# Sandwich block on eight cores: two router loads queued behind two weight slabs, and the second layer norm written into the projection's buffer

## The reference

```python
x = x + _layernorm(_L0_attn_ref(_layernorm(x), Wq, Wk, Wv, Wo))
x = x + _layernorm(_L0_ffn_ref(_layernorm(x), base_W, router_W, lora_A, lora_B))

# attention: Q = x @ Wq.T (32 heads of 128), K = x @ Wk.T, V = x @ Wv.T (one head),
# rotary embedding, windows of 512 tokens that overlap by half:
scores = jnp.einsum('bhqd,bkd->bhqk', Qw, Kw) * scale
attn = jax.nn.sigmoid(scores)
attn = attn / jnp.sum(attn, axis=-1, keepdims=True)
wout = jnp.einsum('bhqk,bkd->bhqd', attn, Vw)      # overlapping windows are blended linearly
return out @ Wo.T

# feed-forward: 8 experts, top 2, adapters of rank 16
base = jnp.einsum('bsd,od->bso', x, base_W)
logits = jnp.einsum('bsd,ed->bse', x, router_W)    # softmax, top 2, renormalised: w_dense
mid = jnp.einsum('bsd,edr->bser', x, lora_A) * w_dense[..., None]
inc = jnp.einsum('bser,erd->bsd', mid, lora_B)
return base + inc * SCALING
```

## Time and profile before

| | |
|---|---|
| median of 3 runs | 2698.13 us (2696.24 to 2703.28) |
| profiled execution, its time | 2701.05 us |
| profiled execution, span of the slowest core (core 4) | 2699.2 us |
| spans of the other cores | 2678.3 to 2691.7 us |
| TensorE matmul, busy | 1951.5 us (72%) |
| ScalarE, busy | 657.0 us (24%) |
| VectorE, busy | 603.9 us (22%) |
| DMA queue of GpSimd | 113.35 MB, 36.3% of the 16 DMA engines' time |

### The profile page before, as it was taken

One profiled execution on the slowest core, in us unless ns is written; L12 is line 12 of the kernel. 1 busy time (PEld: TensorE's weight loads), 2 busy tenths in 40 slices (PEclk: granted clock), 3 DMA queues, 4 the chain that ended last, 5 costly groups with the idle time before them and its releaser, 6 DMA issues.

```text
span 2699.2 us, 49584 instructions; the slowest of 8 cores (2678.3 to 2699.2 us)
## 1 busy us (share of the span) xinstructions
PE 1951.5 (72%) x20000; PEld 1667.1 (62%) x20000; DVE 603.9 (22%) x1752; ACT 657.0 (24%) x1143; POOL 101.9 (4%) x82
## 2 busy tenths in 40 slices
PE   1357999999977777772999999722125999999400
PEld 0237999999755555552888888621124888888400
DVE  2431222222134434431000000133432000000244
ACT  3650111111254554550011111133232111111111
POOL 1000000000000000000000000000000000000000
PEclk9999999999988988885999999855556999999755
DMA  9821445654200000006576776412152676676233
GB/s 201 197 94 33 64 63 75 83 64 64 32 2 2 2 2 2 2 2 53 60 89 68 79 79 70 71 33 63 48 83 43 71 87 70 72 85 71 85 148 140
DMA packets 228587, 178.96 MB, mean 66 GB/s; under 512 B 18960, under 2 KB 222736, under 8 KB 222736
## 3 DMA queue, kind: packets, MB, share of 16 engines
q0 software_dynamic: 217568, 113.35, 36.3%
q1 hardware_dynamic: 10800, 62.45, 6.4%
HBM read 263.97 MB, written 25.17 MB: 107 GB/s over the span
## 4 chain that ended last, share of the span: by engine, by line
PE 64%; DVE 12%; ACT 9%; issue 8%; DMA 7%; DVEq 1%; ACTq 0%; SPq 0%; POOL 0%; POOLq 0%
PE ps_all L768 17%; PE ps_all L653 17%; PE ps_all L443 16%; PE ps_all L541 5%; DVE bn L263 5%; DMA xstage<-x_ext 3%; ACT sig L508 2%; PE ps_all L494 2%; DMA out<-outstage 2%; DMA slab<-woT 2%; DVE bl L575 1%; DVE outstage L794 1%; PE ps_all L295 1%; ACT xt_stage L282 1%; PE ps_all L677 1%
## 5 line engine op out<-in xcount | busy, mean ns | idle before, releaser
L653 PE MATMUL ps_all<-slab,attn_T 128*128 128x256 bf16 x4096 | 449.5, 273 | 46.6 <-DMA slab<-woT 46.6
L443 PE MATMUL ps_all<-slab,ln1T_own 128*128 128x256 bf16 x4096 | 469.6, 273 | 0.6 <-ACT krT L374 0.6
L768 PE MATMUL ps_all<-slab,ln2T 128*128 128x256 bf16 x4096 | 464.0, 274 | 0.2 <-issue 0.2
L653 PEld LDWEIGHTS ps_all<-slab,attn_T 128*128 128x128 bf16 x4096 | 401.9, 98 | 94.1 <-issue 46.7
L768 PEld LDWEIGHTS ps_all<-slab,ln2T 128*128 128x128 bf16 x4096 | 402.1, 98 | 48.1 <-issue 0.3
L443 PEld LDWEIGHTS ps_all<-slab,ln1T_own 128*128 128x128 bf16 x4096 | 396.3, 98 | 45.0 <-issue 0.8
L508 ACT ACTIVATE sig<-ps_all,kbias_s 128x512 bf16<-128x512 f32 x384 | 225.5, 722 | 228.1 <-PE ps_all L494 228.0
L541 PE MATMUL ps_all<-v_sb,sig 128*128 128x128 bf16 x2048 | 204.3, 229 | 75.3 <-DVE bl L584 70.0
L541 PEld LDWEIGHTS ps_all<-v_sb,sig 128*128 128x128 bf16 x2048 | 192.3, 108 | 85.4 <-issue 85.1
L551 PE MATMUL ps_all<-onesc,sig 128*128 128x1 bf16 x2048 | 199.3, 175 | 0.0
L494 PE MATMUL ps_all<-qrT,krT 128*128 128x256 bf16 x768 | 153.3, 317 | 39.7 <-ACT sig L508 35.5
(11 more groups left out here) (86 smaller groups left out, 1494.1 us busy)
## 6 DMA issues: line engine op xcount, KB each, us to landing
slab<-wqT POOLq DMA_DIRECT2D x16, 2048.0 KB, 17.5
slab<-woT POOLq DMA_DIRECT2D x16, 2048.0 KB, 21.9
slab<-baseT POOLq DMA_DIRECT2D x16, 2048.0 KB, 18.8
xstage<-x_ext SPq DMA_DIRECT2D x12, 2048.0 KB, 14.7
out<-outstage SPq DMA_DIRECT2D x8, 2048.0 KB, 6.7
xre<-x_ext POOLq DMA_DIRECT2D x8, 1024.0 KB, 9.9
x_scratch<-x1b SPq DMA_DIRECT2D x8, 1024.0 KB, 4.3
x1re<-x_scratch SPq DMA_DIRECT2D x8, 1024.0 KB, 4.9
```

What stands on the lines that cost most here:

```text
L443: return e.matmul(reg, ln1T_own[:, d, t * 128:(t + 1) * 128], slabs[par][:, d, :], start=(d == 0), stop=(d == 31))
L653: return e.matmul(reg, attn_T[:, d, t * 128:(t + 1) * 128], slabs[par][:, d, :], start=(d == 0), stop=(d == 31))
L768: return e.matmul(reg, ln2T[:, d, t * 128:(t + 1) * 128], slabs[par][:, d, :], start=(d == 0), stop=False)
```

## The change

Two edits. The loads of a_all and routerT leave the place between C and D and are issued on GpSimd after the loads of woT slabs 0 and 1 and before that of slab 2; a_all still waits for C_DONE, routerT follows it in order. FW2_N, the value that the router's matmuls wait for, is the same 32 as before. And E's second layer norm writes into proj[:, t, :], tile t's own part of the projection, instead of xt2stage, which is gone; the wait for earlier transposes to be evicted goes with it.

```diff
-    xt2stage= sb("xt2stage", (128, D), BF16, FREG + 8192)
@@
     s_fw2 = P.sem("s_fw2")
-    P.op("gpsimd", lambda e: e.dma_start(
-            out=a_all_s[:, :, :],
-            in_=a_all.rearrange("(t p) c -> p t c", p=128)),
-         waits=[(s_ate, C_DONE)], inc=s_fw2, inc_by=16)
-    P.op("gpsimd", lambda e: e.dma_start(
-            out=routerT_s[:, :, :],
-            in_=routerT.rearrange("(t p) c -> p t c", p=128)),
-         waits=[(s_ate, C_DONE)], inc=s_fw2, inc_by=16)
-    FW2_N = s_fw2.n
+    FW2_N = 32
 
     p_ring = Ring([ps[0], ps[1], ps[2], ps[3]], init_conds=[(s_ate, C_DONE)])
     pev_counts = {}
     for s in range(NSLAB):
         par, c_slab = emit_slab_load(woT, s)
+        if s == 1:
+            P.op("gpsimd", lambda e: e.dma_start(
+                    out=a_all_s[:, :, :],
+                    in_=a_all.rearrange("(t p) c -> p t c", p=128)),
+                 waits=[(s_ate, C_DONE)], inc=s_fw2, inc_by=16)
+            P.op("gpsimd", lambda e: e.dma_start(
+                    out=routerT_s[:, :, :],
+                    in_=routerT.rearrange("(t p) c -> p t c", p=128)),
+                 inc=s_fw2, inc_by=16)
@@
-        c_ap2 = emit_ln_stats_apply(x1b[tp][:, :], xt2stage[:, :],
-                                    waits=[(s_chain, c_add)],
-                                    extra_apply_waits=[(s_tpe, s_tpe.n)])
+        c_ap2 = emit_ln_stats_apply(x1b[tp][:, :], proj[:, t, :],
+                                    waits=[(s_chain, c_add)])
@@
-        emit_transpose_tile(xt2stage[:, :], dvf, src_waits=[(s_apply, c_ap2)])
+        emit_transpose_tile(proj[:, t, :], dvf, src_waits=[(s_apply, c_ap2)])
```

## The result

| | before | changed |
|---|---|---|
| median of 8 runs | 2697.69 us | 2656.71 us (2654.24 to 2660.46) |
| profiled execution, its time | 2701.05 us | 2656.56 us |
| its span, slowest core | 2699.2 us | 2655.0 us |

The ratio of the times is 0.9848, with a 95% interval of 0.9837 to 0.9859: 41 us less. The forecast was 46.1 us less, so it was right in kind and 5 us too large. The ratio, and every time and ratio of the experiments, leaves out executions in which a die was disturbed; one such is among the eight behind 2697.69, which without it would be 2697.26.

The account below looks back on a forecast made before the run. It took the join of C and D as the bound: slab 0's load queued behind a_all, which waits for C. Terms 45.65 + 0.5 + 0 = 46.1 us brought the median from 2698.13 to 2652.0; range 2646 to 2661.

Parts of the forecast that it names:

- (1): Ahead of stage D on core 4: slabs 0 and 1 load under C at no cost, removing 45.65 us.
- one sign of being wrong in kind: Stage C, the attention: growth by more than a microsecond or two would show the prediction wrong in kind.
- (2): Slab 2's load in D: queue empty 6 us before its issue, 5 us of slack, cost nothing.
- The rival's price of 13.8 us: Stage D: slab 2 lands late behind routerT, TensorE waits 13.8 us, time 2666; chance 0.09.
- the 28 that the prediction named: Loads in stage D: landing times should stay under 28 us after issue.
- (3): D's entry: TensorE's clock still starts low, no gain taken; bounds 2.7 us gained, about 1 us lost.
- The sum: Whole kernel on core 4: 45.65 + 0.5 + 0 = 46.1 us gained, median 2652.0.
- core 4 stays the slowest: End of the kernel: core 4 still ends last, narrowly, with core 6 at 2651.0, 2 us below it.
- the forecast had 0.5: Stage E's second layer norm: 8 applies each lose 0.06 us of wait handling, 0.5 us gained.
- the gain is that of another core: Stall ahead of D: if a core with core 6's 41.2 us is slowest, gain 40.8, time 2657; chance 0.10.

Follow-up runs that it names:

- e5: The changed kernel with each of the two early woT slab loads done seven times under the attention; 2653.9 us, ratio 0.985.
- e8: The changed kernel with a_all and routerT held until slab 0 is multiplied, issued directly ahead of slab 2; 2661.3 us, ratio 0.988.
- e10: The changed kernel with tile t+1's layer norms issued inside tile t's router work, but xt2stage and its wait kept; 2559.2 us, ratio 0.9504.
- e2: The changed kernel with a_all and routerT back ahead of slab 0, so only the layer norm's buffer edit remains; 2691.2 us, ratio 0.9988.
- e6: The changed kernel with a_all alone back ahead of slab 0, routerT after slab 1; 2686.2 us, ratio 0.997.
- e7: The changed kernel with routerT alone back ahead of slab 0, a_all after slab 1; 2685.7 us, ratio 0.9969.
- e4: The changed kernel with slabs 0 and 1 also waiting for the attention's end, still ahead of the router loads; 2678.4 us, ratio 0.9941.

## Why the prediction was right, and where 5 us went

*The stall goes whole* ((1) of the prediction): right. The new gap is 1.1 us; 1241.75 - 1240.80, the end of C's last matmul, had allowed 0.95. Transfers under C cost nothing that can be told, shown at seven times the traffic. The prediction had named one sign of being wrong in kind, an attention longer by more than a microsecond or two. Core 4 showed it, with 4.9 us; the mean of the eight cores, 509.0 against 509.2, and e5 say that it was that core's scatter.

*Slab 2* ((2)): right. No wait of line 653 for a slab is left, and D's loads on core 4 landed in time:

```profile
DMA to landing us min/median/max: 16.7/17.3/18.1
```

The working was cautious: routerT landed 12.1 us after its issue, not 22.5, so the queue was empty 17 us ahead of slab 2 and not 6. The rival's price of 13.8 us was too high; e8 put it at 8.0, a wait of 5.5 and 2.5 of slow clock, which the price had left out. The slack is not large, though: in e10 one core's loads took up to 28.5 us to land in D, past the 28 that the prediction named, and it waited 1.5 us for a slab. No other core of the runs with the new order (but for e8) waited for one.

*The clock* ((3)): right. Windows of the changed kernel at D's entry, beside the earlier trace rows; the clock stands after POOL's busy time.

```profile
1244.00:1246.00 2.00, 0.43 (x3) 0.29 (x3) 1.30 (x6) 0.13 (x1) 0.00 (x0) 0.99 0.00 0
1246.00:1248.00 2.00, 0.92 (x6) 0.49 (x5) 0.19 (x1) 1.06 (x2) 0.14 (x1) 0.50 0.00 0
1248.00:1250.00 2.00, 2.00 (x12) 1.37 (x10) 0.00 (x0) 0.00 (x0) 2.00 (x2) 0.50 0.00 0
1250.00:1252.00 2.00, 2.00 (x11) 1.40 (x10) 0.00 (x0) 0.00 (x0) 1.21 (x1) 0.50 0.03 3
1252.00:1254.00 2.00, 2.00 (x17) 1.61 (x16) 0.00 (x0) 0.11 (x1) 0.00 (x0) 0.81 1.29 106
1254.00:1256.00 2.00, 2.00 (x21) 1.79 (x19) 0.00 (x0) 0.27 (x1) 0.00 (x0) 1.00 1.80 179
```

D starts at 0.50 (1.2 GHz) again and reaches 1.00 (2.4 GHz) after some 6 us. TensorE had been busy for 0.43 of the 2 us ahead of the fall. The ramp comes with the attention's thin end even without the stall; 449.8 us of matmuls in D against 449.5 say the same. The Trainium skill's rule (TensorE: Matmul & The Clock Gate, "HAM oscillation — how this bites in real kernels"), that avoiding the idle gap avoids the ramp, isn't borne out at D's entry: the gap went from 46.6 to 1.1 us and the ramp stayed. The other half of it, that a gap brings the ramp, e8 shows, where dense matmuls lay ahead of waits of 4.0 and 6.9 us.

*The sum*: here the size was off. It took core 4's 46.6 us, the longest stall of the eight in one execution, as the stall of whichever core ends last, and held that "core 4 stays the slowest". It did in the profiled pair, whose times differ by 44.5 us. That close agreement is partly luck: core 4's D began only 39.7 us earlier, and stage E (3.0 us, of which the forecast had 0.5) and what follows F's slab matmuls (1.7 us) happened to be shorter in the second profile. But in 13 timed executions of the kernel before, the slowest core was 4, 1, 2, 2, 0, 5, 2, 7, 0, 7, 2, 3 and 5. The cores' spans in them and in four of the order alone, on the same chip:

| | mean of the 8 spans | slowest of the 8 | difference |
|---|---|---|---|
| before, 13 executions | 2682.3 us | 2692.2 us | 9.9 |
| order alone, 4 executions | 2648.6 us | 2653.6 us | 5.0 |
| gain | 33.7 us | 38.6 us | 4.9 |

The gain has two parts. A core on average gains 34 us. The slowest of eight gains another 5, because the stall was unequal and spread the cores. In the profile before, the attention ended within 9.4 us on the eight cores, and D began between 1269.1 and 1287.4, 18 us apart. In the changed kernel it began between 1233.6 and 1247.7, 14 apart, with nothing added by the wait. The ends of the unequal stall in the profile before are the earlier trace rows and this, of core 5:

```profile
  DMA slab<-woT: 33.5, 1
```

How the stall was unequal tells which term was the right one. Take the cores in the pairs 0 and 1, 2 and 3, 4 and 5, 6 and 7. In all five kernels with the stall, and in all four pairs of each, the core whose attention ended later waited longer for slab 0:

| | mean stall of the later cores of the pairs | of the earlier |
|---|---|---|
| before | 42.6 us | 35.0 us |
| e2 | 40.0 | 33.0 |
| e6 | 33.4 | 29.2 |
| e7 | 31.6 | 24.9 |
| e4 | 24.8 | 19.2 |

That is 20 of 20; over all the ways to pair the eight cores the count is 15 in the mean. So the core that is late gets the long stall, and the late core sets the time. Less the new gap of 1.1, the late cores' stalls are 41.5 us (before) and 38.9 (e2); the times fell by 41 and, in the table above, by 38.6. The right term was neither the mean of the eight stalls, 38.8 less 1.1, nor the longest, 45.65, but the stall of a typical late core. This is read from profiles and fits the times; timed executions show spans only, so it isn't proven for them. Through what one core of a pair delays the other's loads, no run here shows.

My rival "the gain is that of another core" gave 40.8 us and 2657, for a slowest core with core 6's stall of 41.2. Its number came out, and core 6 was the later of its pair; I had given it 0.10. The mean span fell by 34 us, where the profiled stalls less the new gap are 38 (before) and 35 (e2). The profiles of e2 and of the order alone show that the missing part need not be in the stall: their mean spans differ by 32.0 us and their stalls by 35.4, and the rest is a start of C that is 1.1 us later, an attention longer by 0.4 and a stretch behind F's slab matmuls longer by 1.9. Such parts vary by 1 to 2 us from one profiled execution to the next, even in the mean over the cores.

## What to carry to other kernels

A load that waits at the head of an engine's in-order list delays all loads behind it; look for the longest idle time of the issuing engine, and ask of each load behind it whether it needs what the head waits for. When several cores run the same program, don't take a wait from the slowest core of one profile as the gain: read it on all cores, see whether the late ones wait longer, and expect what a typical late core waits. A wait whose releaser precedes the waiter on its own engine holds nothing; what holds the stage is the order in which the engines are given their work.

## What the runs showed of the hardware that I had not expected

A load's time to landing went with the order in which the two cores of a pair came to it. routerT, issued right behind a_all each time, landed 16.5 us after its issue in the mean over the cores before (slabs 0 and 1 issued right behind it), 13.8 in e8 (slab 2 behind it) and 11.0 in the changed kernel (nothing behind it). But the kernel before splits by pairs: on the later core of each pair it took 18.6 to 22.5 us, on the earlier 11.1 to 13.0, with the same loads behind it. In e8 the core that came later to slab 2 had the longer time in each pair too, 15.7 us in the mean against 11.9. So a core's own queue behind the load explains little of it, and the loads that its neighbour has already queued are the likelier reason; no run took the neighbour's loads away.

And seven times the early slab loads under the attention, 204 MB moved by a core where it was 179, changed neither the attention nor the time.
